# Two attentions and two feed-forward stages on one core: one wide product with P's high part, partial sums added at the normalisation

## What is computed

```
# first attention: 16 heads of 64 columns, N = 2048, no mask
Q, K, V = x @ Wq.T + bq, x @ Wk.T + bk, x @ Wv.T + bv
w = softmax(Q @ K.T * scale[h], axis=-1)          # 2048 x 2048 per head
y = x + ((w @ V) @ Wo.T + bo)                     # then a layernorm of y
# second attention: 8 heads of 128 columns, rotary, causal mask
p = softmax(mask(q @ k.T / 128)); r = (p @ v) @ w_ao
```

## Time and profile before

| | |
|---|---|
| Median of 3 runs | 1927.22 us (1925.53 to 1928.65) |
| Span of the profiled execution | 1927.3 us |
| PE busy | 1854.3 us, 96% |
| POOL busy | 1597.5 us, 83% |
| ACT busy | 1548.5 us, 80% |
| DVE busy | 1443.6 us, 75% |
| Chain of work that ended last | PE 87%, DVE 4%, POOL 3%, issue 3%, ACT 2% |
| L1600, L1601, L1603 (first attention, P times V) | 4096 matmuls each |

### The profile page before, as it was taken

The page is one execution under the profiler, slowest core; times in us unless marked ns, Lnnn a source line. Parts: engine busy times, 40 slices in busy tenths (PEclk is TensorE's granted clock), DMA queues, the critical chain, the costliest instruction groups (busy, mean ns, idle before and its releaser), DMA issues.

```text
span 1927.3 us, 55726 instructions
## 1 busy us (share of the span) xinstructions
PE 1854.3 (96%) x23471; PEld 1256.4 (65%) x23471; DVE 1443.6 (75%) x2647; ACT 1548.5 (80%) x1921; POOL 1597.5 (83%) x1025
## 2 busy tenths in 40 slices
PE   4899999999999999999999998779999999999998
PEld 3566666666666666666666665547777777767766
DVE  7798878878878878878878875566767767767652
ACT  4799999999999999999999999646666666666664
POOL 3899999999999999999999999358688787787752
PEclk8999999999999999999999999889999999999999
DMA  6101100100100100100100100100000000000000
GB/s 148 35 11 26 34 15 22 35 17 20 35 19 18 35 19 18 35 19 17 35 23 14 35 2 2 55 1 2 2 1 2 2 2 2 2 1 1 2 2 23
DMA packets 45034, 37.96 MB, mean 20 GB/s; under 512 B 8304, under 2 KB 44144, under 8 KB 44528
## 3 DMA queue, kind: packets, MB, share of 16 engines
q1 hardware_dynamic: 44304, 34.00, 7.0%
q10 hardware_dynamic: 480, 0.39, 0.1%
HBM read 8.15 MB, written 1.05 MB: 5 GB/s over the span
## 4 chain that ended last, share of the span: by engine, by line
PE 87%; DVE 4%; POOL 3%; issue 3%; ACT 2%; DMA 0%; SPq 0%; POOLq 0%; DVEq 0%; ACTq 0%
PE ST L1639 11%; PE ST L1640 11%; PE RING L1520 7%; PE OO L1601 6%; PE OO L1603 6%; PE OO L1600 6%; PE OO L1520 4%; PE ST L1832 3%; PE ST L1838 3%; PE ST L1837 3%; PE ST L1839 3%; POOL PBUF L704 2%; PE OO L1859 2%; PE OO L1861 2%; PE OO L1863 2%
## 5 line engine op out<-in xcount | busy, mean ns | idle before, releaser
L620 POOL TENSOR_TENSOR PAB<-PR,PAB 128x1024 f16<-128x1024 f32 x342 | 724.3, 2134 | 42.3 <-ACT PAB L799 42.2
L799 ACT ACTIVATE PAB<-ST,exp_scale 128x1024 f16<-128x1024 f32 x512 | 567.6, 1109 | 0.0
L1104 DVE TENSOR_REDUCE maxes<-RING 128x1 f32<-128x512 f32 x661 | 439.6, 684 | 122.6 <-PE RING L1520 118.2
L1600 PE MATMUL OO<-VP,PAB 128*128 128x66 f16 x4096 | 446.6, 192 | 2.9 <-POOL PAB L620 2.9
L1601 PE MATMUL OO<-VP,PAB 128*128 128x64 f16 x4096 | 447.1, 193 | 0.0
L1603 PE MATMUL OO<-VP,PAB 128*128 128x66 f16 x4096 | 445.1, 192 | 0.0
L797 ACT ACTIVATE PR<-ST,exp_scale 128x1024 f32<-128x1024 f32 x342 | 381.9, 1117 | 64.7 <-PE ST L1640 61.8
L1600 PEld LDWEIGHTS OO<-VP,PAB 128*128 128x128 f16 x4096 | 380.2, 96 | 78.3 <-issue 15.5
L1601 PEld LDWEIGHTS OO<-VP,PAB 128*128 128x128 f16 x4096 | 377.0, 97 | 60.6
L1639 PE MATMUL ST<-QL,KH 128*128 128x512 f16 x1024 | 388.6, 380 | 2.0 <-DVE QH L1116 1.0
L1640 PE MATMUL ST<-QH,KL 128*128 128x512 f16 x1024 | 388.8, 380 | 0.0
(11 more groups left out here) (319 smaller groups left out, 4027.8 us busy)
## 6 DMA issues: line engine op xcount, KB each, us to landing
KH<-HS SPq DMA_DIRECT2D x124, 64.0 KB, 2.0
QL<-HS SPq DMA_DIRECT2D x64, 64.0 KB, 2.0
QL<-LS SPq DMA_DIRECT2D x64, 64.0 KB, 2.0
QH<-HS SPq DMA_DIRECT2D x64, 64.0 KB, 2.0
KL<-LS SPq DMA_DIRECT2D x62, 64.0 KB, 2.0
X<-in_L_attn_a_x SPq DMA_DIRECT2D x4, 256.0 KB, 4.2
SHARED<-in_rope_cos SPq DMA_DIRECT2D x1, 1024.0 KB, 5.2
SHARED<-in_rope_sin SPq DMA_DIRECT2D x1, 1024.0 KB, 7.3
```

Of the source, the lines that this page charges most:

```text
L620: pool.tensor_tensor(PB[:, s, :], PRA[g % PR_SLOTS], PA[:, s, :], ALU.subtract).then_inc(p_low_ready, 1)
L799: act.activation(PA[:, step % SLOTS_A, :], ST[step % 2][:, :], ACT.Exp, scale=scale).then_inc(sa.exps, 1)
L1104: dve.reduce_max(maxes[:, i // BLOCKS, i % BLOCKS:i % BLOCKS + 1], bank[:, :], X_AXIS).then_inc(sa.ring_taken, 1)
L1600: pe.matmul(o, high, v[:, 0:V2_AT], start=(m == 0 and qt == 0), stop=False, skip_group_check=True)
```

## The change

1. **Layout.** A V row becomes V_low, one column of ones, V_high (64 + 1 + 64 = 129 columns used of 130). In the second attention likewise (128 + 1 + 128); there the first and third matmul get 129 columns in place of 130 and nothing else changes in their number.
2. **pv_a.** For query tiles 0 to 2, P_high is multiplied once with all 129 columns, so that P_high x V_low, the denominator and P_high x V_high stand side by side in PSUM, and P_low is multiplied with the 65 columns from the ones on. For query tile 3 there are three matmuls as before, of 65, 64 and 65 columns. 3 x 129 + 65 = 452 columns lie in the bank O[0].
3. **normalise_a.** The partial sums with V_low now stand apart and have to be added. In place of two instructions there are seven: reciprocal of three denominators, reciprocal of the fourth, (wait) V_low sums of three tiles times the reciprocals into `o_low` (192 columns), (wait) the fourth tile (64 columns, `tensor_scalar`), and three `scalar_tensor_tensor` of 64 columns, each tile times its reciprocal plus `o_low`. The last one counts up `a2_ready`.

```diff
-                link(dve.reciprocal(rden[:, :], o[:, :, 0]))
-                dve.tensor_tensor(A2[:, qb * BT:(qb + 1) * BT, hs * DA:(hs + 1) * DA], o[:, :, V1_AT:V2_AT],
-                                  rden[:, :].unsqueeze(2).broadcast_to((P, BT, DA)), ALU.mult
-                                  ).then_inc(a2_ready, 1)
+                o = O[0][:, 0:O4_AT].rearrange("p (q c) -> p q c", c=WIDE_A)
+                dst = A2[:, qb * BT:(qb + 1) * BT, hs * DA:(hs + 1) * DA]
+                dve.reciprocal(rden[:, 0:3], o[:, :, ONE_AT])
+                link(dve.reciprocal(rden[:, 3:4], O[0][:, O4_AT:O4_AT + 1]))
+                link(dve.tensor_tensor(o_low[:, :, :], o[:, :, 0:DA],
+                                       rden[:, 0:3].unsqueeze(2).broadcast_to((P, 3, DA)), ALU.mult))
+                dve.tensor_scalar(dst[:, 3, :], O[0][:, O4_AT + 1:O4_AT + NARROW_A], rden[:, 3:4], None, ALU.mult)
+                for i in range(3):
+                    ins = dve.scalar_tensor_tensor(dst[:, i, :], o[:, i, V1_AT:V_END], rden[:, i:i + 1],
+                                                   o_low[:, i, :], ALU.mult, ALU.add)
+                ins.then_inc(a2_ready, 1)
...
-                    o = O[0][:, qt * V2_AT:(qt + 1) * V2_AT]
-                    pe.matmul(o, high, v[:, 0:V2_AT], start=(m == 0 and qt == 0), stop=False, skip_group_check=True)
-                    pe.matmul(o[:, V1_AT:V2_AT], high, v[:, V2_AT:VCOL], start=False, stop=False,
-                              skip_group_check=True)
-                    ins = pe.matmul(o, low, v[:, 0:V2_AT], start=False, stop=(m == TILES - 1),
-                                    skip_group_check=True)
+                    first, last = m == 0 and qt == 0, m == TILES - 1
+                    if qt < 3:
+                        o = O[0][:, qt * WIDE_A + ONE_AT:(qt + 1) * WIDE_A]
+                        pe.matmul(O[0][:, qt * WIDE_A:(qt + 1) * WIDE_A], high, v[:, 0:V_END], start=first, stop=False,
+                                  skip_group_check=True)
+                    else:
+                        o = O[0][:, O4_AT:O4_AT + NARROW_A]
+                        pe.matmul(o, high, v[:, ONE_AT:V_END], start=False, stop=False, skip_group_check=True)
+                        pe.matmul(o[:, 1:NARROW_A], high, v[:, 0:DA], start=False, stop=False, skip_group_check=True)
+                    ins = pe.matmul(o, low, v[:, ONE_AT:V_END], start=False, stop=last, skip_group_check=True)
```

More of the change, by code:

```diff
@@ L66 @@
 WCOL = WV_AT + DA
-V1_AT = 2
-V2_AT = V1_AT + DA
-VCOL = V2_AT + DA
-HB, DB = 8, 128
-V1B_AT = 2
-V2B_AT = V1B_AT + DB
-VB = V2B_AT + DB
+ONE_AT = DA
+V1_AT = ONE_AT + 1
+V_END = V1_AT + DA
+VCOL = V_END + 1
+WIDE_A, NARROW_A = V_END, 1 + DA
+O4_AT = 3 * WIDE_A
+HB, DB = 8, 128
+ONEB_AT = DB
+V1B_AT = ONEB_AT + 1
+VB_END = V1B_AT + DB
+VB = VB_END + 1
+OB_WIDE = 1 + DB
 ITER_B = HB // 2
@@ L347, in build @@
         rden = sb("rden", [P, BT])
+        o_low = sb("o_low", [P, 3, DA])
         ones_f = sb("ones_f", [P, P])
@@ L602, in _ @@
             ins.then_inc(consts, 1)
-            pool.memset(VP[:, :, :, 0:V1_AT], 1.0).then_inc(ones_set, 1)
+            pool.memset(VP[:, :, :, ONE_AT:V1_AT], 1.0).then_inc(ones_set, 1)
             for i in range(4):
@@ L871, in values_high_b @@
                 act.wait_ge(sbb.ring_put, item + 1)
-                act.activation(VBS[:, hs, part * BT:(part + 1) * BT, V1B_AT:V2B_AT],
+                act.activation(VBS[:, hs, part * BT:(part + 1) * BT, V1B_AT:VB_END],
                                bank[:, :].rearrange("p (t c) -> p t c", c=DB), ACT.Copy).then_inc(vb_high, 1)
@@ L1085, in take_values_a @@
                 vf = bank[:, :].rearrange("p (t c) -> p t c", c=DA)
-                link(dve.tensor_copy(vp[:, :, V1_AT:V2_AT], vf))
-                dve.tensor_tensor(vp[:, :, V2_AT:VCOL], vf, vp[:, :, V1_AT:V2_AT], ALU.subtract
+                link(dve.tensor_copy(vp[:, :, V1_AT:V_END], vf))
+                dve.tensor_tensor(vp[:, :, 0:DA], vf, vp[:, :, V1_AT:V_END], ALU.subtract
                                   ).then_inc(sa.ring_taken, 1)
@@ L1321, in normalise_b @@
                 three, fourth = OB[ul % 2]
-                o = three[:, 0:3 * V2B_AT].rearrange("p (a c) -> p a c", c=V2B_AT)
+                o = three[:, 0:3 * OB_WIDE].rearrange("p (a c) -> p a c", c=OB_WIDE)
                 dve.reciprocal(rden[:, 0:3], o[:, :, 0])
                 link(dve.reciprocal(rden[:, 3:4], fourth[:, 0:1]))
-                dve.tensor_scalar(AB[:, 3, :], fourth[:, V1B_AT:V2B_AT], rden[:, 3:4], None, ALU.mult
+                dve.tensor_scalar(AB[:, 3, :], fourth[:, 1:OB_WIDE], rden[:, 3:4], None, ALU.mult
                                   ).then_inc(sbb.fourth_taken, 1)
-                dve.tensor_tensor(AB[:, 0:3, :], o[:, :, V1B_AT:V2B_AT],
+                dve.tensor_tensor(AB[:, 0:3, :], o[:, :, 1:OB_WIDE],
                                   rden[:, 0:3].unsqueeze(2).broadcast_to((P, 3, DB)), ALU.mult
@@ L1334, in take_values_b @@
                 v = VBS[:, hs, part * BT:(part + 1) * BT, :]
-                dve.tensor_tensor(v[:, :, V2B_AT:VB], bank[:, :].rearrange("p (t c) -> p t c", c=DB),
-                                  v[:, :, V1B_AT:V2B_AT], ALU.subtract).then_inc(sbb.ring_taken, 1)
+                dve.tensor_tensor(v[:, :, 0:DB], bank[:, :].rearrange("p (t c) -> p t c", c=DB),
+                                  v[:, :, V1B_AT:VB_END], ALU.subtract).then_inc(sbb.ring_taken, 1)
             def settle_ffn(b):
@@ L1854, in pv_b @@
                         wait(pe, sbb.fourth_taken, it * UNITS_B + ul)
-                    bank, at = (OB[ul % 2][0], qt * V2B_AT) if qt < 3 else (OB[ul % 2][1], 0)
-                    o = bank[:, at:at + V2B_AT]
+                    bank, at = (OB[ul % 2][0], qt * OB_WIDE) if qt < 3 else (OB[ul % 2][1], 0)
+                    o = bank[:, at:at + OB_WIDE]
                     tile = slice(qt * P, (qt + 1) * P)
                     high, low = PAH[:, g % SLOTS_B, tile], PAL[:, g % SLOTS_B, tile]
-                    pe.matmul(o, high, v[:, 0:V2B_AT], start=(step == 0 and qt in (0, 3)), stop=False,
+                    pe.matmul(o, high, v[:, ONEB_AT:VB_END], start=(step == 0 and qt in (0, 3)), stop=False,
                               skip_group_check=True)
-                    pe.matmul(o[:, V1B_AT:V2B_AT], high, v[:, V2B_AT:VB], start=False, stop=False,
-                              skip_group_check=True)
-                    ins = pe.matmul(o, low, v[:, 0:V2B_AT], start=False, stop=(step == BT * qb + qt),
+                    pe.matmul(o[:, 1:OB_WIDE], high, v[:, 0:DB], start=False, stop=False, skip_group_check=True)
+                    ins = pe.matmul(o, low, v[:, ONEB_AT:VB_END], start=False, stop=(step == BT * qb + qt),
                                     skip_group_check=True)
```

3 lines of the change are left out of this document (1 added, 2 removed).

## The result

The change makes the kernel slower: 1970.15 us (1970.0 to 1971.27, 4 runs) against 1927.93 us (1925.53 to 1929.01, 4 runs), a ratio of 1.0221, interval 1.0209 to 1.0233. The profiled execution has a span of 1968.2 us (before 1927.3), so 40.9 us more; its own time is 1970.05 us, 1.85 us above its span.

The account below looks back on a forecast made before the run. PE was taken to set the pace, with 0.05 us slack per unit at the hand-over from DVE. 1927.3 + 53.3 + 0.9 (last normalisation) - 9.9 - 0.9 = 1970.7, say 1970 us; range 1952 to 1995.

Parts of the forecast that it names:

- chain of seven on DVE: First attention's normalisation, reciprocal to last sum: 1.54 us in place of 0.63, bounds 1.38 and 1.90 us.
- end of the chain to PE's start: From DVE's last normalisation instruction to PE's first product when PE stands waiting: 0.15 us.
- lost at the borders: PE's first product starts 0.86 us later per unit, 62 times: 53.3 us, bounds 43 and 76.
- wide product: PE matmul of 129 columns in the first attention: 56.5 ns, bounds 55 to 60 ns.
- key tile, before and after: PE's products of one key tile: twelve in 360 ns before, nine in 350 ns afterwards.
- saving of the new products: First attention on PE: 11 ns for 7/8 of 1024 key tiles, 9.9 us, between 0 and 13.4.
- The dear bound: DVE chain with each small instruction held until the one ahead has ended: 1.90 us.
- The exception for step 2: Two of each unit's sixteen key tiles only shorten PE's way to the wait, so 14/16 count.
- The second attention: Two columns less for each of 1088 products: 0.9 us less.
- Rival 1: At the unit's border PE's hidden slack covers the wait and the saving stays: 1916.5 us, partly covered about 1927; 5%.
- Rival 2: Wide products no cheaper: odd PSUM starts slow matmuls, some 2110 or 1991 us, 4%; wide product at 80 ns, 2043 us, 1%.
- Rival 3: PE's stream is bound by something three fewer matmuls don't relieve, saving 0: 1981 us; 10%.

Follow-up runs that it names:

- e1: Kernel before with its old products, but seven vector instructions in the first attention's normalisation, the last three taking a maximum instead of a sum: 1979.33 us, ratio 1.0264.
- e4: Kernel before with the four score matmuls of step 4 issued ahead of a unit's first product: 1942.3 us, ratio 1.0078.
- e3: Changed kernel with the four score matmuls of step 4 issued ahead of a unit's first product: 1935.02 us, ratio 1.0037.
- e2: Changed kernel without the addition of the V_low sums for three of four query tiles, so a normalisation of four instructions: 1927.48 us, ratio 0.9994.
- e5: Changed kernel with each of the three last sums of the normalisation cut into two halves of 32 columns: 1995.35 us, ratio 1.0351.
- e6: Changed kernel with query tiles 130 instead of 129 PSUM columns apart, so that sums of wide products start at even columns: 1971.26 us, ratio 1.0221.
- e9: e3 with the projection or product for V of step 4 issued in step 5: 1928.71 us, ratio 1.0007.
- e7: Changed kernel with the second maximum reduction of step 2 put behind the normalisation on DVE: 1961.77 us, ratio 1.0176.
- e13: Changed kernel with V_low sums copied out, the addition releasing O[0], and the multiplication of 192 columns afterwards from SBUF alone: 2033.43 us, ratio 1.0548.
- e14: e13's early release with the multiplication on POOL, scores of step 4 ahead of the first product, transposition in step 5: 1931.01 us, ratio 1.0018.
- e12: e9 with the splitting of Wo moved from the fifth unit to the sixth: 1929.01 us, ratio 1.0005.

## Why the prediction was right, and where it was not

The forecast was 1970 us and 2.2%; measured were 1970.15 us and a ratio of 1.0221. The mechanism held at each step, but the last digits agree partly by luck.

| step of the sum | forecast | measured |
|---|---|---|
| chain of seven on DVE | 1.54 us | 1.51 us |
| end of the chain to PE's start | 0.15 us | 0.146 us |
| first reciprocal to first product, before and after | 0.83 and 1.69 us | 0.83 and 1.66 us |
| lost at the borders | 62 x 0.86 = 53.3 us | 53.4 us in 63 (before: 0.2) |
| wide product | 56.5 ns | 57.7 ns (mean) |
| key tile, before and after | 360 and 350 ns | 365 and 354 ns (medians of 1024) |
| saving of the new products | 9.9 us | 10.2 us (stream), 9.2 and 7.3 us (e1 - after, e4 - e3) |
| first to last product of the first attention | +43.4 us | +43.8 us |
| the rest of the span | 0 | -2.9 us |

**The chain.** The sum from rows of the same kind was 0.03 us too high: the small instructions followed each other 0.19 us apart (forecast 0.20) and took 275 ns (284). The dear bound, each held until the one ahead had ended, did not occur. The term that would have been easy to miss is the width: the added instructions work on few columns, and their price is their number. The groups on DVE show it (count, mean ns):

```profile
L1209 DVE SCALAR_TENSOR_TENSOR SHARED<-OO,rden,o_low 128x64 f32<-128x64 f32 x192 | 42.2, 275 | 0.0
...
L1205 DVE TENSOR_TENSOR o_low<-OO,rden 128x192 f32<-128x192 f32 x64 | 22.9, 357 | 2.2
```

**The exposure.** That the whole 0.86 us a unit would reach the end was the step on which all hung; it came from the slack of 0.05 us in the earlier trace rows and from the place of the wait in PE's queue. e1 shows the loss with the old products, e2 that as little as 0.18 us more on DVE is already felt, e5 that a longer chain costs nearly one for one. The count was off the other way: I had taken the last border as covered, and it still held 0.57 us: 63 borders with 53.4 us instead of 62 with 53.3. That these agree to 0.1 us is luck.

**The saving.** 10.2 us are in the stream: 3072 starts of 2.2 ns, 6.8 us, and 8 columns less for each of 1024 key tiles, 3.4 us. I had counted 7/8 of 11 ns a tile. The 360 ns that I took for the twelve products of before came from one key tile, and the median is 365; the 350 for the nine was too low by nearly as much, so the difference held. The exception for step 2 (the two tiles that only bring PE to its wait sooner) can't be read apart at this size.

**The second attention and what lies outside.** The forecast was -0.9 and +0.9 us, the trace shows -2.9. Span less first attention is 793.0 us before and 790.1 after, but 790.8 in e1, whose code there is that of before, and 789.7 to 794.4 over all profiled executions. Most of it lies in the second attention, which varies with the same code: from its first to its last product it took 602.2 us in before and 599.0 in after, but 602.3 in e6, whose code there is that of after. So most of the 2.9 us can't be the change's doing, and the 0.9 us of fewer columns are too small to be read. It made the difference of spans 2.5 us smaller than my sum.

**Span and time.** I set the span of 1927.3 equal to the median of 1927.22. The time of an execution lies about 1.8 us above its span, though, in each of the twelve profiled executions of the other kernels, so that a span of 1927.3 would belong to a run of about 1929.1. Which run of before was profiled is not on record; the highest of the four was 1929.01. On the scale of spans the sum, 1970.7, was 2.5 us too high; that 1.8 us were missing between span and time brought it back.

**The rivals.** Rival 1, the wait covered, gave 1916.5; no kernel reached it, but e3 and e9 show what would have been needed, another order of PE's work, and that it brings waits of its own. Rival 2, odd starts or a dear wide product: e6 moves the query tiles to even starts without effect, and the wide products take 57.7 ns. So the rule of the Trainium skill, "TensorE: Matmul & The Clock Gate", section "Back-to-back issue gap", with about 81 ns for weight load and matmul of 128 columns in a stream, does not hold in this trace; 57.7 ns for 129 columns is near its figure for an isolated one. Rival 3, no saving: excluded by e1 with 9.2 us.

**My expectations behind the prediction were worse than the prediction.** In e3, e7, e9, e13 and e14 the removed wait was priced about rightly and the next one, or its size, not seen; in e4 there was none to remove, and the same new one came. In e3 and e4 it was a ring bank claimed 0.86 us sooner, in e7 the transposition's wait for the held maxima (4.7 us), in e9 and e14 the bank of the item that had been moved (3.3 and 4.8 us), in e13 DVE's stand beside POOL, which the expectation had as its rival and at 1955 or more. e12 removed 2.6 us in the trace and nothing in the median.

## What to carry to other kernels

A saving on the engine that sets the pace is worth what it measures only as long as nothing is added to the chain that hands it its buffer: here some 10 ns a key tile saved on PE were to be paid with 0.9 us on DVE per unit, at a place where the slack was 0.05 us. Read the slack at each hand-over (end of the releasing instruction, plus the release latency from a place where the engine really stood waiting, to the start of the waiting one) before adding instructions there, and price small ones by their number, not by their columns. When such a wait is moved away by another order, look at once for the bank or buffer that is now asked for sooner; four orders of this kernel (e3, e4, e9, e14) each brought a new such claim. And measure from start to start, since the small ones are in no list of waits.

## What the runs showed of the hardware

**A multiplication on DVE that reads only SBUF waits for POOL's instruction to end.** In e13 the same 192 columns took 357 ns at the least, at the median 2159 ns, and 1.9 us on average; the copy and the addition of the same width, which read at least one operand from PSUM, took 348 ns with POOL at work beside them all 64 times. At the median DVE is held up by 2159 - 357 = 1.80 us. The Trainium skill, "SBUF — State Buffer", section "Who interferes with whom", says of this that a DVE instruction with two inputs in SBUF contends with a GpSimd instruction that reads SBUF, that the port pair which they share is an exclusive lock, and that a DVE instruction with at most one input there, outside the 2-port perf modes, does not contend. The trace agrees, with 2159 against 348 ns. It means here that moving DVE's work off PSUM, to release PSUM earlier, can cost more than it frees. The trace also shows the order. In all 64 cases the multiplication ends 0.21 to 0.26 us after the end of the POOL instruction that was running when it started, whenever it started: the seven of 357 to 360 ns began only some 0.1 us ahead of that end, those of the median's length 1.9 us ahead, and five of 0.67 to 1.87 us in between. POOL's next instruction is held in its turn: where it starts more than 0.1 us ahead of the multiplication's end (62 times), it ends 1.98 to 2.00 us behind that end and is drawn 2.24 to 2.30 us long instead of 2.13. So in this trace the one that comes second is held by the one that is under way.

**A drawn matmul hides a wait.** The list of waits gave 0.2 us in e2, where 9.3 us were lost in 62 gaps of 0.14 us at the median, because a matmul is drawn 0.38 us long and occupies PE for 0.216. Gaps under 0.16 us are seen only from start to start.

**Small instructions on DVE.** 32 columns took 243 ns, 64 columns 275, and 192 columns (as `tensor_tensor`) 357: halving the width saved 32 ns of each.
